# Head scores of a cross-conditioned attention layer as fp32 products in row quarters, in place of stacked high and low parts

## The chip, the cores and the metric

The kernel runs on one core of a Trainium2 chip. The metric is the device time of one execution in microseconds (us); three executions were timed. The engines are called PE (TensorE, with PEld its weight loads), DVE (VectorE), ACT (ScalarE), POOL (GpSimd) and SP (SyncE).

## What is computed

The input x is 64 sequences x 128 positions x 512 features, float32. It goes through two layers; only the second is changed. Its core, from the reference (16 heads of 32 features, B = 64, T = 128):

```python
xn = layer_norm(x, norm_w, norm_b)
q = (xn @ q_w + q_b).reshape(Bx, Tx, H, -1)
k = (xn @ k_w + k_b).reshape(Bx, Tx, H, -1)
att = jnp.einsum('bnhl,bmhl->bnmh', q, k)
att = att + (1.0 - mask) * -1000000.0
att = jax.nn.softmax(att, axis=2)
v = ((xn @ v_w + v_b) * src_mask[:, :, None]).reshape(Bx, Tx, H, -1)
y = jnp.einsum('bnmh,bmhl->bnhl', att, v).reshape(Bx, Tx, Dx)
h = layer_norm(y, sb_norm_w, sb_norm_b) * (1.0 + scale) + shift
return x + jax.nn.silu(h) @ out_w + out_b
```

The first layer has the same frame around a linear attention of 8 heads.

## The kernel before

A setup stage prepares weights, layer 1 (`layer0`) runs over 32 pairs of sequences, then layer 2 (`layer1`) does. Every engine has its own program, written out by hand; semaphores join them (`wait_ge`, `then_inc`). Layer 2 is a software pipeline: `body(i)` projects pair i and finishes pair i - 1. There are 32 bodies and an end for the last pair. b is the sequence in the pair, c a chunk of 128 features (four heads), a the head's place in its chunk, which is also its quarter of 32 partitions.

Each projection is three passes (`project_rows` L457 to L450, `project_features`; PE rows L448 to L450 and L457 to L459): high times high, low times high, high times low, in fp32r. Twelve matmuls make one projection of 512 columns (values or output, of one sequence) and twelve of 256 columns one chunk of the keys or queries of both.

The head scores use the same three parts, but one head has only 32 features, so the parts are stacked on the partitions. `qk_high` (ACT, L1302) takes each chunk of keys and queries out of PSUM as fp32r, and `qk_low` (DVE, L1168) what is left of it. 25 DMAs of a pair (`restack` on SP, `query_low_rows` on ACT) copy the parts into `stack`: high, high and low of the keys against high, low and high of the queries, 96 rows, then two rows of the mask and one of the shift. One matmul of 98 rows by 128 columns then gives a head's scores with its mask (`scores`, L1498). DVE takes the negated row maxima (`maxima`, L1176, each over one PSUM bank of four heads). `shift_row` (L1508) transposes them, ACT copies them and a DMA puts them in row 98 of the stack (`shift_out`). `weight_scores` (L1456) computes the scores a second time, keys on the partitions, shifted by the maximum, and `exps` (ACT, L1315) makes the weights out of them. So each pair has 2 x 16 matmuls of scores and 2 x 16 of weight scores, 128 x 128 each.

`mixed` (L1465, L1471) applies the weights: fp32 products with 32 output partitions, four at once in the column quarters of the array. `turned` (L1482), `z_transposed` (L1415) and `x_transposed` (L1405) transpose.

PE's order in a body: keys 0 and 1, with `shift_row` of sequence 1 of the previous pair in between; weight scores of sequence 0; keys 2 and 3; weight scores 1; queries 0 and 1; `mixed` 0; queries 2 and 3; `mixed` 1; values 0 (with `turned` between); z 0; values 1 (with x transposes); z 1; then the scores and the two output projections woven matmul by matmul. Scores of sequence 1 go to the same banks as those of sequence 0, so they wait for the maxima; DVE alternates maxima with its other work.

## Time and profile before

| | us |
|---|---|
| three timed runs: lowest, median, highest | 2303.02, 2305.43, 2308.46 |
| the profiled execution | 2304.43 |
| its span in the trace | 2302.6 |
| PE busy in the span | 2232.5 (97%) |
| DVE busy | 1458.1 (63%) |
| ACT busy | 871.8 (38%) |
| POOL busy | 569.1 (25%) |

The busy time of PE is modelled at the ends of matmuls, which overlap, so a stream is read from the starts of its rows in the timeline, not from their durations. In the 40 slices of the page PE is at 9 tenths or more in nearly all of them, in both layers. The chain that ended last is PE for 48% of the span in named rows, and no other engine has more than 2%.

### The profile page before, as it was taken

To read this page: it belongs to the slowest core of one execution; us is meant where nothing else is said; L and a number is where in the kernel's file an instruction comes from. 1 tells how busy PE (TensorE), PEld (TensorE's weight loads), DVE (VectorE), ACT (ScalarE), POOL (GpSimd) and SP (SyncE) were. 2 spreads that over 40 slices of the span, in tenths; PEclk is the share of its full clock that TensorE was granted. 3 is DMA by queue.
4 is the path that set the end of the run, shared out by engine and by line. 5 is a ranking of instruction groups with operands and counts; after the bars stand their busy time and mean duration, and the time that the engine had idled before them with its cause. 6 is when DMAs were issued, how large, how long until landed. Compare 5 with 4: busy or idle time off the path is not lost.

```text
span 2302.6 us, 49399 instructions
## 1 busy us (share of the span) xinstructions
PE 2232.5 (97%) x18430; PEld 1953.2 (85%) x18430; DVE 1458.1 (63%) x3127; ACT 871.8 (38%) x2021; POOL 569.1 (25%) x847
## 2 busy tenths in 40 slices
PE   6999999999999999995999999999999999999997
PEld 2888888888888888884989898989898988888886
DVE  4677777777777777745565656565656565555554
ACT  2333333333333333322344444444444444444443
POOL 0332223333333333313212121212122121212120
PEclk9999999999999999987999999999999999999998
DMA  7201111110100011003354444444444535353532
GB/s 247 86 32 37 37 37 37 37 37 37 37 30 34 32 37 37 32 24 88 81 123 105 116 112 114 114 107 117 107 122 101 128 101 129 94 129 92 129 87 72
DMA packets 90934, 187.17 MB, mean 81 GB/s; under 512 B 18708, under 2 KB 29394, under 8 KB 90904
## 3 DMA queue, kind: packets, MB, share of 16 engines
q1 hardware_dynamic: 82712, 169.44, 26.9%
q10 hardware_dynamic: 8192, 17.31, 3.2%
q8 instruction: 20, 0.33, 0.1%
q14 instruction: 10, 0.08, 0.0%
HBM read 51.81 MB, written 33.69 MB: 37 GB/s over the span
## 4 chain that ended last, share of the span: by engine, by line
PE 48%; ACT 2%; DVE 2%; SPq 1%; DMA 1%; issue 1%; POOL 0%; DVEq 0%; POOLq 0%
PE bank L457 6%; PE bank L459 5%; PE bank L458 5%; PE bank L1456 5%; PE bank L449 5%; PE bank L448 5%; PE bank L450 5%; PE bank L1498 4%; PE bank L1465 3%; PE bank L1471 2%; PE bank L1482 1%; SPq L1052 1%; PE bank L1405 1%; PE bank L1415 1%; ACT g L1332 1%; DMA stack<-parts 1%
## 5 line engine op out<-in xcount | busy, mean ns | idle before, releaser
L457 PE MATMUL bank<-xT_hi,w_hi 128*128 128x256 f32 x1536 | 444.7, 290 | 2.6 <-DVE xT_lo L1159 1.4
L458 PE MATMUL bank<-xT_lo,w_hi 128*128 128x256 f32 x1536 | 441.6, 287 | 0.0
L459 PE MATMUL bank<-xT_hi,w_lo 128*128 128x256 f32 x1536 | 439.0, 286 | 0.0
L448 PE MATMUL bank<-w_hi,xT_hi 128*128 128x512 f32 x768 | 322.7, 420 | 0.0
L450 PE MATMUL bank<-w_lo,xT_hi 128*128 128x512 f32 x768 | 317.8, 414 | 0.0
L449 PE MATMUL bank<-w_hi,xT_lo 128*128 128x512 f32 x768 | 311.8, 406 | 0.0
L457 PEld LDWEIGHTS bank<-xT_hi,w_hi 128*128 128x128 f32 x1536 | 291.1, 189 | 10.8 <-issue 6.1
L1168 DVE SCALAR_TENSOR_TENSOR parts<-bank,qk_bias,parts 128x256 fp32r<-128x256 f32 x256 | 111.1, 475 | 294.4 <-ACT parts L1302 294.4
L458 PEld LDWEIGHTS bank<-xT_lo,w_hi 128*128 128x128 f32 x1536 | 292.3, 190 | 1.7
L459 PEld LDWEIGHTS bank<-xT_hi,w_lo 128*128 128x128 f32 x1536 | 291.4, 190 | 0.0
L448 PE MATMUL bank<-w_hi,h_hi 128*128 128x512 f32 x512 | 217.6, 425 | 3.6 <-DVE h_lo L1218 3.6
L449 PE MATMUL bank<-w_hi,h_lo 128*128 128x512 f32 x512 | 215.8, 421 | 0.0
L805 ACT ACTIVATE k_exp<-bank,k_neg 128x128 f32<-128x128 f32 x256 | 73.0, 370 | 370.7 <-DVE k_neg L690 368.7
L1498 PEld LDWEIGHTS bank<-stack 98*128 98x128 f32 x1024 | 173.9, 194 | 46.4 <-DVE top L1176 21.1
L450 PE MATMUL bank<-w_lo,h_hi 128*128 128x512 f32 x512 | 210.4, 411 | 0.0
L1302 ACT ACTIVATE parts<-bank,qk_bias 128x256 fp32r<-128x256 f32 x256 | 107.5, 471 | 236.2 <-PE bank L459 236.2
L1498 PE MATMUL bank<-stack 98*128 98x128 f32 x1024 | 172.5, 268 | 10.1 <-DMA stack<-parts 8.1
L450 PEld LDWEIGHTS bank<-w_lo,xT_hi 128*128 128x128 f32 x768 | 144.6, 188 | 39.5
L1108 POOL TENSOR_TENSOR xr<-xr,bias_all 128x512 f32 (+1 forms) x64 | 81.1, 1289 | 392.3 <-DVE top L1176 391.4
L448 PEld LDWEIGHTS bank<-w_hi,xT_hi 128*128 128x128 f32 x768 | 144.6, 188 | 38.9 <-DVE parts L1168 6.2
L1176 DVE TENSOR_REDUCE top<-bank 128x4 f32<-128x512 f32 x256 | 169.9, 683 | 9.1 <-PE bank L1498 9.0
L449 PEld LDWEIGHTS bank<-w_hi,xT_lo 128*128 128x128 f32 x768 | 145.2, 189 | 30.5
(173 smaller groups left out, 4191.9 us busy)
## 6 DMA issues: line engine op xcount, KB each, us to landing
stack<-parts SPq DMA_DIRECT2D x640, 128.0 KB
xr<-in_x SPq DMA_DIRECT2D x32, 512.0 KB, 3.5
x_between_layers<-x SPq DMA_DIRECT2D x64, 256.0 KB, 2.0
xr<-x_between_layers SPq DMA_DIRECT2D x32, 512.0 KB, 3.6
stack<-parts ACTq DMA_DIRECT2D x128, 128.0 KB
out<-y_out SPq DMA_DIRECT2D x64, 256.0 KB, 2.0
raw<-in_L_cond_W_emb SPq DMA_DIRECT2D x4, 1024.0 KB, 12.2
raw<-in_L_cond_emb_w SPq DMA_DIRECT2D x4, 1024.0 KB, 7.6
```

The source lines that it names most:

```text
L448: yield nc.tensor.matmul(bank[:, :], a_hi[:, c, b, :], w_hi[:, m, c, :], start=(c == 0), stop=False)
L449: yield nc.tensor.matmul(bank[:, :], a_lo[:, c, b, :], w_hi[:, m, c, :], start=False, stop=False)
L450: yield nc.tensor.matmul(bank[:, :], a_hi[:, c, b, :], w_lo[:, m, c, :], start=False, stop=(c == C - 1))
L457: yield nc.tensor.matmul(dst, w_hi[:, m, c, fs], a_hi[:, c], start=(first and c == 0), stop=False)
L458: yield nc.tensor.matmul(dst, w_hi[:, m, c, fs], a_lo[:, c], start=False, stop=False)
L459: yield nc.tensor.matmul(dst, w_lo[:, m, c, fs], a_hi[:, c], start=False, stop=(c == C - 1))
L1108: last = nc.gpsimd.tensor_tensor(xr[:, slot, b], xr[:, slot, b], bias_all[:, BO, :], ALU.add)
L1168: nc.vector.scalar_tensor_tensor(parts[:, LO[n], c].rearrange("p b t -> p (b t)"), ps[QK_BANKS[n][c // 2]][:, at:at + PAIR * P], qk_bias[: ...
L1176: nc.vector.tensor_reduce(top[:, b, :].rearrange("p (a c) -> p a c", c=C)[:, :, j], ps[S_BANKS[j]][:, :].rearrange("p (h t) -> p h t", h=H ...
L1302: nc.scalar.activation(parts[:, HI[n], c].rearrange("p b t -> p (b t)"), ps[QK_BANKS[n][c // 2]][:, at:at + PAIR * P], ACT.Identity, bias= ...
L1456: last = nc.tensor.matmul(ps[W_BANKS[j]][:, a * P:(a + 1) * P], stack[0:K_SHIFTED, 1, a, j, b, :], stack[0:K_SHIFTED, 0, a, j, b, :], star ...
L1498: last = nc.tensor.matmul(ps[S_BANKS[j]][:, a * P:(a + 1) * P], stack[0:K_SCORE, 0, a, j, b, :], stack[0:K_SCORE, 1, a, j, b, :], start=Tr ...
```

## The change

The keys and queries are taken out of PSUM once each, in full fp32, into `qk`: the keys by DVE (`keys_out`), the queries by ACT (`queries_out`). A head's scores are one fp32 matmul of 32 rows by 128 columns, read from the partitions where the projection left the head, in the row quarter `tile_position=(DH * a, 0)` of the array (`heads`). The four heads of a chunk, in four quarters, write to four banks. A bank now holds one quarter's four heads. The mask is added first, by one matmul per bank with two rows of ones against `mask_rows`, 512 columns wide; the shift likewise, by four rows of ones against `top_T`, which ACT writes in four copies, each with a column of zeros and ones (`chunk_of`) as its scale. In the weight scores the mask is the bias of the exponentials (`mask_add`). The `stack`, its DMAs and `qk_low` are gone. `top` is padded to 128 columns, so the transposed maxima lie in the quarters.

The order changes too. The first scores follow z 0, ahead of values 1. The second scores stand between the two output projections, as a block. Nothing is woven there. The transposes of x stand before output projection 0 and after it. The banks of values, z, outputs and shift rows change with it. DVE normalises the next pair before it takes out the keys; `keys_out` waits until the weight scores of the previous pair are done. The setup gets one transpose and one copy (`mask_off`).

The core of the diff (waits and names around it follow in kind; `exps`, `maxima` and `mixed` keep their number of instructions):

```diff
-    parts = sb(ctx, "parts", [P, 4, C, PAIR, P], F32R)
-    Q_LO, Q_HI, K_HI, K_LO = range(4)
-    HI, LO = (Q_HI, K_HI), (Q_LO, K_LO)
-
-    stack = sb(ctx, "stack", [P, 2, HC, C, PAIR, P], F32R)
+    qk = sb(ctx, "qk", [P, 2, C, PAIR, P])
+    mask_rows = sb(ctx, "mask_rows1", [P, PAIR * P], F32R)
+    mask_add = sb(ctx, "mask_add", [P, PAIR])
+    one_rows = sb(ctx, "one_rows", [P, P], F32R)
+    chunk_of = sb(ctx, "chunk_of", [P, DH])
     v = sb(ctx, "v1", [P, PAIR, H, DH])
     one_col = sb(ctx, "one_col", [P, C, DH])
-    top = sb(ctx, "top", [P, PAIR, H])
-    top_T = sb(ctx, "top_T", [H, PAIR, P], F32R)
+    top = sb(ctx, "top", [P, PAIR, P])
+    top_T = sb(ctx, "top_T", [P, PAIR, C, P], F32R)
...
-    V_BANKS = (2, 3)
+    V_BANKS = (4, 6)
     S_BANKS = (0, 1, 2, 3)
     S_ORDER = ((0, 1, 2, 3), (2, 3, 0, 1))
-    Z_BANKS = (4, 5)
-    O_BANKS = (4, 5)
+    Z_BANKS = (5, 4)
+    O_BANKS = (5, 4)
     X_BANKS = (7, 6)
-    T_BANKS = (7, 6)
-    Z_AFTER = 11
+    T_BANKS = (7, 0)
...
-            def rows(side, part, r):
-                for a in range(HC):
-                    sp.dma_start(f32(stack[DH * r:DH * r + DH, side, a]),
-                                 f32(parts[DH * a:DH * a + DH, part])).then_inc(s["stack"], 16)
...
+        def load_masks(pair):
+            for a in range(HC):
+                sp.dma_start(f32(mask_rows[DH * a:DH * a + 2, :]),
+                             mask_d[1, :, bass.ds(pair * PAIR, PAIR)].rearrange("r b t -> r (b t)"))\
+                    .then_inc(s["masks_in"], 16)
...
+        def keys_out(i, first):
+            if not first:
+
+                dve.wait_ge(s["w_ps"], seq(PAIR * C, i - 1, PAIR * C))
+            for c in range(C):
                 if c % 2 == 0:
-
-                    dve.wait_ge(s["qk_hi"], seq(2 * C, i, (1 - n) * C + c + 2))
+                    dve.wait_ge(s["qk_ps"], seq(C, i, c // 2 + 1))
                 at = (c % 2) * PAIR * P
-                nc.vector.scalar_tensor_tensor(
-                    parts[:, LO[n], c].rearrange("p b t -> p (b t)"), ps[QK_BANKS[n][c // 2]][:, at:at + PAIR * P],
-                    qk_bias[:, n, c:c + 1], f32(parts[:, HI[n], c]).rearrange("p b t -> p (b t)"), ALU.add,
-                    ALU.subtract).then_inc(s["qk_lo"], 1)
+                done = nc.vector.tensor_scalar(qk[:, K, c].rearrange("p b t -> p (b t)"),
+                                               ps[QK_BANKS[K][c // 2]][:, at:at + PAIR * P], qk_bias[:, K, c:c + 1],
+                                               None, ALU.add)
+                if c % 2:
+                    done.then_inc(s["k"], 1)
...
         def body(i, first, more, last):
-            qk_low(i, 1, range(C))
             if not last:
                 row_stats(i + 1, (i + 1) % RING)
-            qk_low(i, 0, (0, 1))
+                norm(i + 1, (i + 1) % RING)
+            keys_out(i, first)
             if not first:
                 end_outputs(i - 1, 0)
-            qk_low(i, 0, (2, 3))
-            if not last:
-                norm(i + 1, (i + 1) % RING)
-            if not first:
                 end_norm(i - 1, 0)
                 end_outputs(i - 1, 1)
...
+        def exps(prev, b):
+            if b == 0:
+                act.wait_ge(s["mask_add"], seq(1, prev, 1))
             for a in range(HC):
-                act.dma_start(f32(stack[DH:2 * DH, 0, a]),
-                              f32(parts[DH * a:DH * a + DH, Q_LO])).then_inc(s["stack"], 16)
-
-        def exps(prev, b):
-            for j in range(C):
-                act.wait_ge(s["w_ps"], seq(PAIR * C, prev, b * C + j + 1))
-                nc.scalar.activation(prob[:, b, HB * j:HB * j + HB, :],
-                                     ps[W_BANKS[j]][:, :].rearrange("p (h t) -> p h t", h=HB),
-                                     ACT.Exp).then_inc(s["prob"], 1)
+                act.wait_ge(s["w_ps"], seq(PAIR * C, prev, b * C + a + 1))
+                nc.scalar.activation(prob[:, b].rearrange("p (c a) t -> p c a t", c=C)[:, :, a, :],
+                                     ps[W_BANKS[a]][:, :].rearrange("p (c t) -> p c t", c=C),
+                                     ACT.Exp, bias=mask_add[:, b:b + 1]).then_inc(s["prob"], 1)
...
         def shift_out(i, b):
             act.wait_ge(s["top_ps"], seq(PAIR, i, b + 1))
-            nc.scalar.activation(top_T[:, b, :], ps[T_BANKS[b]][0:H, 0:P], ACT.Copy).then_inc(s["top_T"], 1)
-            act.wait_ge(s["top_T"], seq(PAIR, i, b + 1))
-            act.dma_start(f32(stack[ROW_SHIFT:ROW_SHIFT + 1, 0, :, :, b, :]).rearrange("o a c t -> o (a c) t"),
-                          f32(top_T[:, b, :])).then_inc(s[f"shift{b}"], 16)
-
+            for c in range(C):
+                done = nc.scalar.activation(top_T[:, b, c, :], ps[T_BANKS[b]][:, 0:P], ACT.Copy,
+                                            scale=chunk_of[:, c:c + 1])
+            done.then_inc(s["top_T"], 1)
...
+        def heads(dst, weights, moving, b, order, signal):
+
+            for c in range(C):
+                for a in order:
+                    rows = slice(DH * a, DH * a + DH)
+                    last = nc.tensor.matmul(ps[dst[a]][:, c * P:(c + 1) * P], qk[rows, weights, c, b, :],
+                                            qk[rows, moving, c, b, :], start=False, stop=(c == C - 1),
+                                            tile_position=(DH * a, 0))
+                    if c == C - 1:
+                        last.then_inc(signal, 1)
+
         def weight_scores(prev, b):
...
-            pe.wait_ge(s[f"shift{b}"], seq(16, prev, 16))
-            for j in range(C):
-                if b == 0 and j < 2:
-
-                    pe.wait_ge(s["out"], seq(PAIR, prev, j + 1))
-                if b == 0 and j == 2:
-
-                    pe.wait_ge(s["top_T"], seq(PAIR, prev, PAIR))
-                if b == 1:
-                    pe.wait_ge(s["prob"], seq(PAIR * C, prev, j + 1))
-                for a in range(HC):
-                    last = nc.tensor.matmul(ps[W_BANKS[j]][:, a * P:(a + 1) * P], stack[0:K_SHIFTED, 1, a, j, b, :],
-                                            stack[0:K_SHIFTED, 0, a, j, b, :], start=True, stop=True)
-                last.then_inc(s["w_ps"], 1)
+            pe.wait_ge(s["top_T"], seq(PAIR, prev, b + 1))
+            if b == 0:
+
+                pe.wait_ge(s["out"], seq(PAIR, prev, PAIR))
+            else:
+                pe.wait_ge(s["prob"], seq(PAIR * C, prev, C))
+            for a in range(HC):
+                rows = slice(DH * a, DH * a + C)
+                nc.tensor.matmul(ps[W_BANKS[a]][:, :], one_rows[rows, :],
+                                 top_T[rows, b].rearrange("p c t -> p (c t)"), start=True, stop=False,
+                                 tile_position=(DH * a, 0))
+            heads(W_BANKS, K, Q, b, range(HC), s["w_ps"])
...
-        def scores(i, b, banks):
+        def scores(i, b, first):
 
             if b == 0:
-                pe.wait_ge(s["stack"], seq(16 * STACK_DMAS, i, 16 * STACK_DMAS))
-            for j in banks:
-                if b == 0 and j >= 2:
-
-                    pe.wait_ge(s["v"], seq(PAIR, i, j - 1))
-                if b == 1:
-                    pe.wait_ge(s["top"], seq(PAIR * C, i, j + 1))
-                for a in range(HC):
-                    last = nc.tensor.matmul(ps[S_BANKS[j]][:, a * P:(a + 1) * P], stack[0:K_SCORE, 0, a, j, b, :],
-                                            stack[0:K_SCORE, 1, a, j, b, :], start=True, stop=True)
-                    if a == HC - 1:
-                        last.then_inc(s["s_ps"], 1)
-                    if a % 2:
-                        yield
+                pe.wait_ge(s["masks_in"], seq(16 * HC, i, 16 * HC))
+                pe.wait_ge(s["q"], seq(2, i, 2))
+                pe.wait_ge(s["k"], seq(2, i, 2))
+            else:
+                pe.wait_ge(s["top"], seq(PAIR * C, i, C))
+            for a in S_ORDER[b]:
+                rows = slice(DH * a, DH * a + 2)
+                nc.tensor.matmul(ps[S_BANKS[a]][:, :], one_rows[rows, :],
+                                 mask_rows[rows, b * P:(b + 1) * P].unsqueeze(1).broadcast_to([2, C, P]),
+                                 start=True, stop=False, tile_position=(DH * a, 0))
+            heads(S_BANKS, Q, K, b, S_ORDER[b], s["s_ps"])
...
-            woven(values1, () if last else x_transposed(i + 1, first))
+            scores(i, 0, first)
+            run(value_rows(i, 1, first))
             if first:
                 pe.wait_ge(s["preset"], 2)
-            outputs0, scores0 = () if first else out_rows(i - 1, 0), scores(i, 0, S_ORDER[0])
+            pe.wait_ge(s["v"], seq(PAIR, i, 1))
             if not first:
                 z_transposed(i - 1, 1)
-            run(islice(scores0, 4))
-            woven(outputs0, scores0)
-            outputs1, scores1 = () if first else out_rows(i - 1, 1), scores(i, 1, S_ORDER[1])
-            woven(outputs1, scores1, 6)
+            if not last:
+                x_transposed(i + 1, 0)
+            if not first:
+                run(out_rows(i - 1, 0))
+            if not last:
+                pe.wait_ge(s["v"], seq(PAIR, i, PAIR))
+                x_transposed(i + 1, 1)
+            scores(i, 1, first)
+            outputs1 = () if first else out_rows(i - 1, 1)
+            run(islice(outputs1, 6))
             if not last:
 
                 pe.wait_ge(s["xT_lo"], seq(PAIR, i + 1, 1))
             shift_row(i, 0)
-            woven(outputs1, scores1)
+            run(outputs1)
```

What stands on PE now and stood there before, at the second scores (a body of the loop). `bank<-stack` are head scores, `h_hi` and `h_lo` the activations of the output projection, `qk` keys and queries. Before:

```order
L448 MATMUL bank<-w_hi,h_hi 128x512 [waits l1_h_lo]
L1496 REGISTER_ALU
L1498 MATMUL bank<-stack 128x128 [waits l1_top]
L1498 MATMUL bank<-stack 128x128
L449 MATMUL bank<-w_hi,h_lo 128x512
L1498 MATMUL bank<-stack 128x128 x2
L450 MATMUL bank<-w_lo,h_hi 128x512
L1498 MATMUL bank<-stack 128x128 [waits l1_top]
L1498 MATMUL bank<-stack 128x128
L448 MATMUL bank<-w_hi,h_hi 128x512
L1498 MATMUL bank<-stack 128x128 x2
```

With the change:

```order
L1386 MATMUL bank<-ident,xn 128x128 x3
L1485 MATMUL bank<-mask_rows,one_rows 128x512 [waits l1_top]
L1485 MATMUL bank<-mask_rows,one_rows 128x512 x3
L1427 MATMUL bank<-qk 128x128 x16
L453 MATMUL bank<-w_hi,h_hi 128x512 [waits l1_h_lo]
L454 MATMUL bank<-w_hi,h_lo 128x512
L455 MATMUL bank<-w_lo,h_hi 128x512
L453 MATMUL bank<-w_hi,h_hi 128x512
L454 MATMUL bank<-w_hi,h_lo 128x512
L455 MATMUL bank<-w_lo,h_hi 128x512
L1493 MATMUL bank<-ident,top 128x128 [waits l1_top,l1_xT_lo]
```

Eight of the scores' matmuls stand here ahead of, and between, single matmuls of the output projection; with the change sixteen stand as one block ahead of it, behind four 512 columns wide, and wait for all maxima of sequence 0.

PE at the weight scores of sequence 0 before, the last row being the next keys:

```order
L1456 MATMUL bank<-stack 128x128 [waits l1_out,l1_shift0]
L1456 MATMUL bank<-stack 128x128 x3
L1456 MATMUL bank<-stack 128x128 [waits l1_out]
L1456 MATMUL bank<-stack 128x128 x3
L1456 MATMUL bank<-stack 128x128 [waits l1_top_T]
L1456 MATMUL bank<-stack 128x128 x7
L457 MATMUL bank<-xT_hi,w_hi 128x256 [waits l1_top]
L458 MATMUL bank<-xT_lo,w_hi 128x256
```

With the change, from the last matmul of keys 1:

```order
L464 MATMUL bank<-xT_hi,w_lo 128x256
L1443 MATMUL bank<-top_T,one_rows 128x512 [waits l1_out,l1_top_T]
L1443 MATMUL bank<-top_T,one_rows 128x512 x3
L1427 MATMUL bank<-qk 128x128 x16
L462 MATMUL bank<-xT_hi,w_hi 128x256 [waits l1_top]
```

The sixteen matmuls, until now in groups of four per bank, follow four of the shift.

DVE at the head of a loop body before (`ISA` and `REGISTER_ALU` rows work out semaphore values):

```order
L1168 SCALAR_TENSOR_TENSOR parts<-bank,qk_bias,parts 128x256 [waits l1_qk_hi]
L1168 SCALAR_TENSOR_TENSOR parts<-bank,qk_bias,parts 128x256
L1166 REGISTER_ALU
L1168 SCALAR_TENSOR_TENSOR parts<-bank,qk_bias,parts 128x256 [waits l1_qk_hi]
L1168 SCALAR_TENSOR_TENSOR parts<-bank,qk_bias,parts 128x256
L1142 ISA
L1144 ISA [waits l1_x_in]
L1144 BN_STATS stats<-xr 128x6
L1144 ISA
L1144 BN_STATS stats<-xr 128x6
L1145 ISA
L1146 COPY seen<-eps 128x1 [waits l1_stats]
```

With the change, from the end of the next pair's statistics:

```order
L1137 ISA
L1138 COPY seen<-eps 128x1 [waits l1_stats]
L1140 BN_AGGR mv<-stats 128x2 x2
L1144 REGISTER_ALU
L1146 TENSOR_SCALAR xn<-xr,mv,rstd 128x512 [waits l1_rstd]
L1146 TENSOR_SCALAR xn<-xr,mv,rstd 128x512
L1157 ISA
L1160 ISA [waits l1_w_ps]
L1162 TENSOR_SCALAR qk<-bank,qk_bias 128x256 [waits l1_qk_ps]
L1162 TENSOR_SCALAR qk<-bank,qk_bias 128x256
L1160 REGISTER_ALU
L1162 TENSOR_SCALAR qk<-bank,qk_bias 128x256 [waits l1_qk_ps]
```

The normalisation of the next pair, which waits for POOL's `rstd`, stands ahead of the keys now, and the keys wait for the previous weight scores; their low parts are gone.

## Rows read from the trace of the kernel before

**Rows 1.** The page: the span, and busy time, share and instructions of each engine.
```profile
span 2302.6 us, 49399 instructions
PE 2232.5 (97%) x18430; PEld 1953.2 (85%) x18430; DVE 1458.1 (63%) x3127; ACT 871.8 (38%) x2021; POOL 569.1 (25%) x847
```

**Rows 2.** A stretch: length; busy PE, PEld, DVE, ACT, POOL; PEclk; DMA; GB/s.
```profile
1400.00:1700.00 300.00, 299.47 (x2904) 268.28 (x2903) 173.42 (x358) 126.72 (x288) 63.28 (x104) 1.00 0.46 113
```

**Rows 3.** Timeline, PE (start, us, row): scores and output projections of a body.
```profile
1505.57 0.60 PE L1415 MATMUL bank<-ident,z 128*128 128x128 f32 x4
1506.00 1.11 PE L1498 MATMUL bank<-stack 98*128 98x128 f32 x8
...
1509.06 0.40 PE L450 MATMUL bank<-w_lo,h_hi 128*128 128x512 f32 x1
...
1510.70 0.40 PE L448 MATMUL bank<-w_hi,h_hi 128*128 128x512 f32 x1
...
1514.00 0.27 PE L1508 MATMUL bank<-ident,top 128*16 128x128 f32 x1
...
1515.96 0.28 PE L457 MATMUL bank<-xT_hi,w_hi 128*128 128x256 f32 x1
```

**Rows 4.** Timeline, PE: the weight scores, and the next body's shift row.
```profile
1518.94 1.90 PE L1456 MATMUL bank<-stack 99*128 99x128 f32 x16
1520.67 0.33 PE L457 MATMUL bank<-xT_hi,w_hi 128*128 128x256 f32 x1
...
1551.74 0.27 PE L1508 MATMUL bank<-ident,top 128*16 128x128 f32 x1
```

**Rows 5.** Timeline, PE, layer 1: fp32 products on the whole array, next row.
```profile
714.88 1.95 PE L950 MATMUL bank<-att,qT 128*128 128x130 f32 x16
716.83 0.38 PE L907 MATMUL bank<-mask_rows,key_bias 128*128 x1
```

**Rows 6.** Timeline, PE: fp32 products in column quarters, and the neighbours around them.
```profile
1528.13 0.28 PE L459 MATMUL bank<-xT_hi,w_lo 128*128 128x256 f32 x1
1528.34 1.08 PE L1465 MATMUL bank<-prob,v 128*32 128x128 f32 x32
1529.24 1.06 PE L1471 MATMUL bank<-prob,one_col 128*32 128x128 f32 x32
1530.22 0.38 PE L457 MATMUL bank<-xT_hi,w_hi 128*128 128x256 f32 x1
1530.45 0.28 PE L458 MATMUL bank<-xT_lo,w_hi 128*128 128x256 f32 x1
```

**Rows 7.** Groups by line: busy us, mean ns; idle before.
```profile
L1498 PEld LDWEIGHTS bank<-stack 98*128 98x128 f32 x1024 | 173.9, 194 | 46.4 <-DVE top L1176 21.1 <-issue 5.7 <-DMA stack<-parts 3.4
L1465 PEld LDWEIGHTS bank<-prob,v 128*32 128x32 f32 x2048 | 52.1, 109 | 8.6
```

**Rows 8.** Timeline, PEld, layer 1: loads of 64 columns into two column halves.
```profile
712.52 1.01 PEld L940 LDWEIGHTS bank<-v,k_rows 128*64 128x64 f32 x32 [0.36 <-issue]
```

**Rows 9.** Timeline, PE: waits for the stacked copies, first and last pair.
```profile
1091.95 6.74 PE L1498 MATMUL bank<-stack 98*128 98x128 f32 x28 [5.38 <-DMA stack<-parts]
...
2261.43 1.11 PE L1498 MATMUL bank<-stack 98*128 98x128 f32 x8 [1.08 <-DMA stack<-parts]
```

**Rows 10.** Timeline, PE, ACT and DVE: from transposed z to h_lo, one sequence.
```profile
1539.18 0.60 PE L1415 MATMUL bank<-ident,z 128*128 128x128 f32 x4
1539.81 1.51 ACT L1332 ACTIVATE g<-bank,gains 128x128 f32<-128x128 f32 x4 [3.19 <-PE bank L1415]
...
1543.44 0.69 DVE L1218 TENSOR_TENSOR h_lo<-hs,h_hi 128x512 fp32r<-128x512 f32 x1 [0.70 <-ACT h_hi L1342]
```

**Rows 11.** Page, groups by line: the maxima, out of PSUM.
```profile
L1176 DVE TENSOR_REDUCE top<-bank 128x4 f32<-128x512 f32 x256 | 169.9, 683 | 9.1 <-PE bank L1498 9.0
```

**Rows 12.** Timeline, POOL: its work behind the last maxima of a pair.
```profile
1516.12 2.54 POOL L1108 TENSOR_TENSOR xr<-xr,bias_all 128x512 f32 x2 [12.30 <-DVE top L1176]
...
1518.86 2.04 POOL L1115 TENSOR_TENSOR v_bias<-bias_all,mask_now 128x512 f32<-128x512 f32 x2
```

More of the change, by code:

```diff
@@ L335, in _ @@
             last.then_inc(cond_ps, 1)
+            pe.wait_ge(mask_step, 4)
+            nc.tensor.transpose(ps[EMB_BANKS[1]][:, 0:B], mask_in[:, 1, :], ident[0:B, 0:B]).then_inc(mask_ps, 1)
             pe.wait_ge(vec_ready, 1)
@@ L1117, in biases, with mask_column @@
             last.then_inc(s["v_bias"], 1)
+        def mask_column(pair, first):
+            if not first:
+                pool.wait_ge(s["prob"], seq(PAIR * C, pair - 1, PAIR * C))
+            nc.gpsimd.tensor_copy(mask_add[:], mask_off[:, bass.ds(pair * PAIR, PAIR)]).then_inc(s["mask_add"], 1)
+        nc.gpsimd.memset(f32(one_rows[:]), 1.0).then_inc(s["rows_preset"], 1)
         norm(0)
-        pool.wait_ge(s["rstd"], 1)
-        nc.gpsimd.memset(f32(stack[ROW_MASK:ROW_MASK + 3]), 1.0).then_inc(s["rows_preset"], 1)
-        pool.wait_ge(s["rows_preset"], 1)
         def body(i, first, more, last):
@@ L1132, in body @@
                 end_rstd(i - 1, 1)
+            mask_column(i, first)
         bodies(pool, NP, body)
@@ L1229, in _ @@
         row_stats(0, 0)
+        nc.vector.memset(top[:], 0.0)
+        nc.vector.reduce_sum(chunk_of[:], ident[:].rearrange("p (a r) -> p r a", a=HC), AX_X)
         nc.vector.memset(one_col[:], 0.0).then_inc(s["preset"], 1)
@@ L1397, in _, with x_transposed @@
     def _(pe):
-        def x_transposed(pair, first):
-            for b in range(PAIR):
-                pe.wait_ge(s["xn"], seq(PAIR, pair, b + 1))
-                if not first:
-                    pe.wait_ge(s["y"], seq(PAIR, pair - 2, PAIR))
-                for c in range(C):
-                    last = nc.tensor.transpose(ps[X_BANKS[b]][:, c * P:(c + 1) * P], xn[:, b, c * P:(c + 1) * P],
-                                               ident[:])
-                    if c == C - 1:
-                        last.then_inc(s["xT_ps"], 1)
-                    yield
+        def x_transposed(pair, b):
+            pe.wait_ge(s["xn"], seq(PAIR, pair, b + 1))
+            for c in range(C):
+                last = nc.tensor.transpose(ps[X_BANKS[b]][:, c * P:(c + 1) * P], xn[:, b, c * P:(c + 1) * P], ident[:])
+            last.then_inc(s["xT_ps"], 1)
         def z_transposed(prev, b):
@@ L1433, in projected, with value_rows @@
                     done.then_inc(s["qk_ps"], 1)
-        def value_rows(i, b):
-            pe.wait_ge(s["qk_lo"], seq(2 * C, i, 2 * (b + 1)))
+        def value_rows(i, b, first):
+            if not first:
+                pe.wait_ge(s["y"], seq(PAIR, i - 1, b + 1))
             done = None
@@ L1531, in body @@
                 mixed(i - 1, 1)
-            values0 = value_rows(i, 0)
+            values0 = value_rows(i, 0, first)
             run(islice(values0, 4))
```

117 lines of the change are left out of this document (50 added, 67 removed).

## The prediction

> **What bounds the kernel now.** I read the page first: PE is busy for 97% of the span, DVE for 63% [rows 1]. Then a stretch of layer 2 by itself: in 300 us PE is busy for 299.5, DVE for 173 and ACT for 127, at a granted clock of 1.00 [rows 2]. So layer 2 is as long as what PE has to issue. The next two views are PE's timeline. One `shift_row` stands at 1514.00 and the next at 1551.74 [rows 3, 4]: a body takes 37.74 us. The reader should see in the rows between them what each step takes from start to start, for the durations overlap. An output projection issues seven matmuls in 1.64 us, 0.234 each, for 512 columns [rows 3]. The first 24 matmuls of the next body and a transpose take 2.98 us [rows 3, 4], so one of 256 columns takes 0.12. Four transposes take 0.43 [rows 3].
>
> **What the scores cost now.** From the transposes of z to the next body there are 10.39 us [rows 3]. Less the transposes (0.43), 24 output matmuls (5.62) and the shift row (0.11), 4.23 us are left for the 32 first scores. The weight scores take 1.73 us for sixteen [rows 4], 3.46 for both sequences. Together 7.69 us of each body. Sixteen in 1.73 is 0.108 each, though 128 columns at 0.12 for 256 would be 0.06: here the weight load of 128 columns sets the pace. At 0.108, 32 first scores would be 3.46, so 0.77 of their 4.23 is waiting. Most of that has a row: PEld waited 21.1 us in all for `top`, 0.66 per pair [rows 7].
>
> **What a block of scores costs after the change.** There are four per pair. Each holds four matmuls of 512 columns (mask or shift) and sixteen heads, in rounds of four quarters. No row of this trace shows a product in a row quarter, so each part comes from the nearest row.
> - *A round of four heads.* The nearest row is the same product turned by 90 degrees: fp32, 128 columns, four at once in column quarters. Thirty-two of them take 0.90 us [rows 6], 0.1125 a round. On the whole array with 128-column weights, an fp32 product of 130 columns takes 1.95/16 = 0.122 [rows 5]. So fp32 costs twice the time of fp32r per column, and the load of 128 columns hides behind it. Four rounds: 0.45. The other end is no overlap of the quarters at all: sixteen times 0.108 [rows 4], 1.73.
> - *Are the loads concurrent?* A head loads 128 columns, where a column quarter loads 32. The two lengths are 194 and 109 ns [rows 7], 0.89 ns a column, so 64 columns need about 57 ns. In layer 1, 32 loads of 64 columns, in two column halves, stand in 1.01 us [rows 8], 28 ns from start to start. Loads to different parts of the array overlap there. I take the same for rows; it is the one assumption that the result hangs on.
> - *The wide matmuls.* At best four at once, 0.234 [rows 3]; at worst one after another, 0.94. I take 0.234, by the same assumption.
> - *Entering and leaving the tiled form.* From the last 256-column matmul before the column quarters to the second after them is 2.32 us [rows 6]. Less sixteen rounds (1.80) and two matmuls (0.24), 0.28 are left. A load of 128 columns in place of 32 adds 0.085 [rows 7]: 0.37.
>
> Sum of a block: 0.37 + 0.234 + 0.45 = 1.05 us, 4.2 for a pair instead of 7.69: 3.49 less.
>
> **What the order adds.** Nothing is woven now, so each wait has to be covered by whole steps.
> - *Output projection 0* waits for `h_lo`. That chain takes 4.95 us now, from the start of z's transposes to the end of `h_lo` (1539.18 to 1544.13) [rows 10]. After the change, z 0, a block, values 1, z 1 and x 0 stand in between: 0.43 + 1.05 + 2.81 + 0.43 + 0.43 = 5.15. But DVE has two maxima and a normalisation inside the chain, 0.68 a maximum [rows 11], and any of them can be in the way. I take 0.25 us of stall, between 0 and 0.7.
> - *Second scores* wait for all four maxima of sequence 0. Since the first block PE has values, three sets of transposes and a projection, 6.9 us. DVE has eight operations, about 5.4 at 0.68. Covered by 1.5.
> - *Weight scores 1* wait for all four exponentials of sequence 0; keys 2 and 3 (2.9 us) cover them by some 0.5. *Weight scores 0* wait for the last `end_add`, 2.9 us of keys behind it. Covered.
> - *POOL and DVE at the head of a body.* POOL's biases start when the maxima are in and end 4.8 us later [rows 12]. `rstd` comes behind them, so DVE stands in `norm` for some 6 us and then takes out the keys, with whatever stands behind them. The first taker on PE is the first scores, some 21 us into the body. If the cover went, a late key would cost PE one for one.
> - *ACT* gets six more copies a pair, for the eight of `shift_out` replace two, and loses the four chunks of keys; it has 127 busy of 300 us [rows 2]. DVE loses eight operations and gets four. SP loses 21 DMAs a pair and gets four small ones, due a body later; ACT's queue loses six. The padded shift rows may cost 0.05 each: 0.1 a pair.
>
> So a body loses 3.49 - 0.35 = 3.14 us: 34.6 instead of 37.74. Times 32: 100 us.
>
> **The ends.** With the stack go PE's waits for it in the first and last pair, 5.38 and 1.08 us [rows 9]. The setup gets a transpose and a copy, some 0.3, and the last pair's weight scores wait for exponentials. Together with what these waits delay I take 8 us less, between 4 and 14, since what stood behind them moves up too. Sum: 2302.6 - 100 - 8 = 2194.6 of span, 2196.4 for that execution, and the median of the three runs is 1 us above it: **2197 us**.
>
> **The rivals.**
> - *Overlap, but incomplete.* The quarters' results go to four banks at once, which no row shows. If a round is 1.3 times as long, so are the wide ones: a block gets 0.13 + 0.07 us longer, a pair 0.8, and the time is 2197 + 26 = 2223. For it: nothing. Against it: column quarters lose almost nothing [rows 6], but they share one bank. The Trainium skill ("TensorE: Matmul & The Clock Gate", table of measured speedups in Part 3) has 3.07 times for four row quarters of 512 columns instead of 4, which is this factor of 1.3. Chance 0.11.
> - *A quarter can't load while it multiplies.* Then a round is a load and a product in turn, 0.225 us, a block is 1.50, a pair 1.8 longer: 2255. Against it: the scores now load 128 columns for 194 ns in the very rows that are multiplying, and still start each 0.108 [rows 4, 7]. The same skill page ("The mechanism", Part 3) says that a load overlaps a running matmul only where the row group differs; by the rows this isn't so on the whole array. The page "FP8 and Floating Point Precision" ("TensorE Precision Notes") gives fp32 four passes, which would come to about the same time; the trace shows two times the fp32r time [rows 5, 6]. Chance 0.08.
> - *The block order stalls PE.* If the `h_lo` chain comes 0.7 late, and the shift row or the next keys wait another 0.7 for maxima that DVE reaches late, a body is 1.2 longer than forecast: 2235. DVE's 173 of 300 us speak against it [rows 2]. Chance 0.05.
> - *The quarters take turns* (the other side). If weights of different row groups come in over one path, sixteen loads of 128 columns stay sixteen times 0.108, and the wide matmuls come one by one: 0.37 + 0.94 + 1.73 = 3.04 a block, 12.2 a pair against 7.69 now. A body is 4.8 longer with the stall: 2304.4 + 155 - 8 = 2451. It decides from about 80 ns per head upwards: there a block reaches 1.9 us and the gain is gone. For it: a head has the same 128 columns to load and to stream as now, so without overlap nothing is saved, and the trace shows overlap for columns alone. Chance 0.11.
>
> **How the numbers follow.** The forecast has the remaining 0.65. The range goes down to 2165: no stall at all (11 us), tiled form entered and left for half the price (24). Up it takes in incomplete overlap, stalls and the doubled round, with 10 us over: 2265. Only the quarters that take turns lie outside. About 0.2% is what a measurement of this kernel tells from no change. Slower is the last rival, 0.11; that the cases should meet at no change, 0.02; faster 0.87.
>
> **What would show it.** PE's timeline should have blocks of 1.05 us: four wide matmuls within a few ns of each other, then sixteen heads over 0.45, in steps of four per 0.11. Shift rows of one kind should stand 34.6 us apart. `parts` and `stack` are gone, DVE waits for `rstd` at a body's head, and the granted clock stays at 1.00 in layer 2. PE's wait before output projection 0 is under 0.7. If a head starts each 0.03 us and the time is above 2230, PE's waits on DVE were misjudged; if a head starts each 0.06 or 0.11, the assumption on the row quarters was wrong, and the time says by how much.

## The result and the profile after

| | before | with the change |
|---|---|---|
| median of the timed runs, us | 2306.94 (2303.02 to 2309.18) | 2240.9 (2240.46 to 2241.82) |
| span of the profiled execution | 2302.6 | 2240.0 |
| one body of layer 2 | 37.74 | 35.98 |

The ratio is 0.9716, with a 95% interval of 0.9699 to 0.9733. The kernel is faster, and the time lies in the range; but the gain is 66 us where 108 were forecast. The change was run again beside the second set of experiments:

> The change itself, on the same chip as the three beside it: 2241 us.

Measured: 2239.93 us, ratio 0.9716 (0.9702 to 0.9729).

The page of the changed kernel, to read beside [rows 1]:

```profile
span 2240.0 us, 53652 instructions
PE 2180.2 (97%) x20991; PEld 1883.2 (84%) x20991; DVE 1400.3 (63%) x3001; ACT 906.7 (40%) x2086; POOL 549.0 (25%) x879
```

And its stretch of layer 2, beside [rows 2] (length; busy PE, PEld, DVE, ACT, POOL; PEclk; DMA; GB/s):

```profile
1400.00:1700.00 300.00, 300.00 (x3646) 262.91 (x3646) 174.16 (x347) 141.90 (x319) 60.72 (x115) 1.00 0.08 29
```

PE is still the bound, and more so: 300.00 of 300 us busy at full clock. The instruction count of PE rose from 18430 to 20991, which is the first thing that doesn't fit: per pair the program has 64 head matmuls as before, 16 wide ones and nothing else new. That makes 512 more, and the setup has one transpose more, but the count rose by 2561. The other 2048 are in the next view. It is PE's timeline (start, us, row) with the shift rows of two bodies and one block of weight scores, beside [rows 3, 4, 6]:

```profile
1517.63 0.27 PE L1493 MATMUL bank<-ident,top 128*128 128x128 f32 x1
...
1521.98 0.28 PE L464 MATMUL bank<-xT_hi,w_lo 128*128 128x256 f32 x1
1522.20 0.50 PE L1443 MATMUL bank<-top_T,one_rows 4*128 4x512 f32 x4
1522.53 1.06 PE L1427 MATMUL bank<-qk 32*128 32x128 f32 x32
1523.53 0.38 PE L462 MATMUL bank<-xT_hi,w_hi 128*128 128x256 f32 x1
1523.75 0.28 PE L463 MATMUL bank<-xT_lo,w_hi 128*128 128x256 f32 x1
...
1553.61 0.27 PE L1493 MATMUL bank<-ident,top 128*128 128x128 f32 x1
```

Sixteen head products stand as 32 rows. The groups by line (busy us, mean ns of one) say the same: 64 sequences x 2 x 16 heads are 2048 products, and the trace has

```profile
L1427 PE MATMUL bank<-qk 32*128 32x128 f32 x4096 | 136.7, 271 | 0.0
L1427 PEld LDWEIGHTS bank<-qk 32*128 32x128 f32 x4096 | 137.0, 187 | 4.8
```

Then the same count has to be made for the rows of before that I took the price from. `mixed` issues 16 matmuls of each kind per sequence, 1024 in all, and layer 1 issues four products of 130 columns per sequence, 256 in all. Groups by line of the kernel before:

```profile
L1465 PE MATMUL bank<-prob,v 128*32 128x128 f32 x2048 | 69.2, 276 | 0.0
L950 PE MATMUL bank<-att,qT 128*128 128x130 f32 x512 | 62.8, 275 | 0.5 <-DVE att L725 0.5
```

Twice the number, too. Every fp32 product is two rows, each with a weight load of its own. A timeline row "x32" was sixteen products, and I had read it as 32.

**Where the 62.6 us of span came from.** Three stretches between the same `shift_row` (of sequence 0) of the first and the last pair. Timeline of before, then of the changed kernel (the end with what PE waits for in brackets):

```profile
1098.49 0.41 PE L1508 MATMUL bank<-ident,top 128*16 128x128 f32 x1
...
2268.84 0.27 PE L1508 MATMUL bank<-ident,top 128*16 128x128 f32 x1
```

```profile
1085.16 0.33 PE L1493 MATMUL bank<-ident,top 128*128 128x128 f32 x1
...
2200.71 0.27 PE L1493 MATMUL bank<-ident,top 128*128 128x128 f32 x1
2203.32 0.51 PE L1443 MATMUL bank<-top_T,one_rows 4*128 4x512 f32 x4 [0.78 <-DVE y_out L1222]
...
2207.34 0.80 PE L1443 MATMUL bank<-top_T,one_rows 4*128 4x512 f32 x4 [2.63 <-ACT prob L1305]
...
2211.16 1.08 PE L1453 MATMUL bank<-prob,v 128*32 128x128 f32 x16 [1.31 <-ACT prob L1305]
```

Up to the first: 13.3 us less (1098.49 to 1085.16). Two things went with the stack. One is its fill in the setup. Timeline of POOL and DVE before, then DVE with the change, with the first normalisation of layer 2:

```profile
1055.61 7.68 DVE L1154 TENSOR_SCALAR xn<-xr,mv,rstd 128x512 f32<-128x512 f32 x2 [0.75 <-POOL rstd L1100]
1055.63 6.92 POOL L1122 MEMSET stack<- 3x8192 f32 x1
```

```profile
1056.74 1.01 DVE L1146 TENSOR_SCALAR xn<-xr,mv,rstd 128x512 f32<-128x512 f32 x2 [0.30 <-POOL rstd L1088]
```

Beside POOL's fill of 6.92 us DVE takes 7.68 us for what takes it 1.01 with the change, and PE's first row of layer 2 stands at 1062.89 before and at 1057.35 now, 5.5 us earlier. (The run below that keeps the stack has the 7.68 us, too; no run takes out the fill alone.) The other 7.8 us hold the wait of 5.38 us for the stacked copies [rows 9] and the clock behind it, less some waits that only the change has (twice 0.5 us). Before, PE is busy for 1.62 of the 7 us up to 1092.00, and from there to 1098.50 the granted clock is 0.50, the lower of its two levels (1.2 GHz in place of 2.4): its first 28 matmuls of scores take 6.5 us, where sixteen in the loop take 1.73. With the change the clock is 1.00 at its first scores.

Thirty-one bodies: 1170.35 us before, 1115.55 now, 54.8 less, 1.77 each. Behind the last: 33.8 before, 39.3 now, 5.5 more; PE waits there for `end_add` (0.78) and twice for exponentials (2.63 and 1.31), with no keys of a next pair as cover. Sum: 62.6.

### The profile page after: what moved, and what is told of

Read it like the earlier page. It is cut to its first block, busy times and chain, and to the rows that moved or that the text cites. A ratio compares the mean times of both kernels' runs of the same rounds, so it can differ in the third digit from the quotient of the medians.

```text
span 2240.0 us, 53652 instructions
## 1 busy us (share of the span) xinstructions
PE 2180.2 (97%) x20991; PEld 1883.2 (84%) x20991; DVE 1400.3 (63%) x3001; ACT 906.7 (40%) x2086; POOL 549.0 (25%) x879
## 4 chain that ended last, share of the span: by engine, by line
PE 51%; DVE 1%; ACT 0%; issue 0%; DMA 0%; POOL 0%; POOLq 0%; DVEq 0%; SPq 0%
PE bank L462 6%; PE bank L453 6%; PE bank L463 6%; PE bank L464 5%; PE bank L455 5%; PE bank L454 5%; PE bank L1427 5%; PE bank L1453 3%; PE bank L1459 3%; PE bank L1470 2%; PE bank L1443 1%; PE bank L1393 1%; PE bank L1386 1%; PE bank L1485 1%; PE bank L1493 0%; ACT prob L1305 0%
## 5 line engine op out<-in xcount | busy, mean ns | idle before, releaser
L455 PE MATMUL bank<-w_lo,xT_hi 128*128 128x512 f32 x768 | 309.7, 403 | 0.0
L454 PE MATMUL bank<-w_hi,xT_lo 128*128 128x512 f32 x768 | 306.6, 399 | 0.0
L454 PE MATMUL bank<-w_hi,h_lo 128*128 128x512 f32 x512 | 206.9, 404 | 0.0
L455 PE MATMUL bank<-w_lo,h_hi 128*128 128x512 f32 x512 | 203.5, 397 | 0.0
L1305 ACT ACTIVATE prob<-bank,mask_add 128x512 f32<-128x512 f32 x256 | 154.9, 688 | 100.1 <-PE bank L1427 100.1
L1136 DVE BATCH_NORM_STATS2 stats<-xr 128x6 f32 (+1 forms) x64 | 41.2, 685 | 186.8 <-DMA xr<-x_between_layers 186.5
L1322 ACT ACTIVATE g<-bank,gains 128x128 f32<-128x128 f32 x256 | 96.1, 456 | 142.3 <-PE bank L1393 142.3
L606 POOL TENSOR_TENSOR h_lo<-hs,h_hi 128x512 fp32r<-128x512 f32 x64 | 86.9, 1379 | 236.9 <-ACT h_hi L836 236.9
```

The source lines that it names most:

```text
L454: yield nc.tensor.matmul(bank[:, :], a_lo[:, c, b, :], w_hi[:, m, c, :], start=False, stop=False)
L455: yield nc.tensor.matmul(bank[:, :], a_hi[:, c, b, :], w_lo[:, m, c, :], start=False, stop=(c == C - 1))
L606: nc.gpsimd.tensor_tensor(h_lo[:, :, b, :], hs[:, b], f32(h_hi[:, :, b, :]), ALU.subtract).then_inc(s["h_lo"], 1)
L1305: nc.scalar.activation(prob[:, b].rearrange("p (c a) t -> p c a t", c=C)[:, :, a, :], ps[W_BANKS[a]][:, :].rearrange("p (c t) -> p c t", c=C),
L1322: last = nc.scalar.activation(g[:, b, c, :], ps[Z_BANKS[b]][:, c * P:(c + 1) * P], ACT.Identity, scale=gains[:, 0, c, b:b + 1], bias=gains ...
```

## The experiments

Times are medians; the change itself is at 2241 or, in the second set, at 2240. All came with runs of the kernel before on the same chip (2305.5 to 2308).

### Head products in fp32r

```diff
-    qk = sb(ctx, "qk", [P, 2, C, PAIR, P])
+    qk = sb(ctx, "qk", [P, 2, C, PAIR, P], F32R)
```

> The change with the keys and queries in fp32r instead of fp32, so the head products are single-pass and their low parts are left out of the result; nothing else differs. Theory A (the prediction counted an fp32 product as one traced matmul, while each is two rows of 0.11 us: 32 rows for 16 heads): a block shows 16 head rows in four steps of 0.11, 0.44 us less than now, 1.78 a pair, 57 us in all: 2184 us. Theory B (a quarter cannot load weights while it multiplies): the number of rows stays 32, or the steps stay eight long for sixteen rows, about 2240 us. Theory C (weight loads of different quarters queue up): 16 rows 0.1 us apart, 1.7 us a block, slower than 2300 us.

Measured: 2185.93 us, ratio to before 0.9474 (0.9458 to 0.9489). Timeline of PE, one block:

```profile
1505.37 0.51 PE L1443 MATMUL bank<-top_T,one_rows 4*128 4x512 f32 x4
1505.71 0.57 PE L1427 MATMUL bank<-qk 32*128 32x128 f32 x16
1506.21 0.39 PE L462 MATMUL bank<-xT_hi,w_hi 128*128 128x256 f32 x1
```

Sixteen rows for sixteen heads, and from the first head to the next keys 0.50 us, where the change has 1.00 (1522.53 to 1523.53). Four blocks are 2.0 us shorter, but a body (34.2 us between shift rows) only 1.8: ahead of output projection 0 PE now stands 0.2 us, for `h_lo` (PEld waits 6.1 us for it in all). Twice the rows for fp32 is worth 55 us of the kernel's time. That is the whole distance between 2241 and the forecast of 2197, and 11 us more. Theory A holds. Theories B and C fall: a quarter loads the next weights while it multiplies, and the quarters' loads of 128 columns run side by side.

### Quarter by quarter

```diff
-            for c in range(C):
-                for a in order:
+            for a in order:
+                for c in range(C):
```

> The same products as the change, but all four heads of one quarter in a row, then the next quarter. Theory A (four quarters work at once, and a quarter's own load hides behind its product): 32 rows one after another at 0.11 us, 3.5 us instead of 0.89 a block, 2.65 more for each of 128 blocks: 2241 + 340 = 2580 us. If a load could not hide behind the product of its own quarter: 0.21 us a row, 6.8 a block, about 3000 us. If the overlap of quarters had brought nothing: 2241 us.

Measured: 2477.85 us, ratio 1.0738 (1.0717 to 1.076). Timeline of PE, one block:

```profile
1505.63 0.51 PE L1485 MATMUL bank<-mask_rows,one_rows 2*128 2x512 f32 x4
1505.96 2.71 PE L1427 MATMUL bank<-qk 32*128 32x128 f32 x32
1508.61 0.50 PE L453 MATMUL bank<-w_hi,xT_hi 128*128 128x512 f32 x1
```

The heads take 2.65 us to the next step instead of 1.00, 1.65 more; 128 times that is 211 of the 237 us. My 2580 was too high: strictly one row after another would be 3.5 us, and it was 2.65. The starts in the trace show why. Rows of one quarter start 0.11 us apart, though each has a load of its own of 187 ns, so a load does hide behind the product of its own quarter. But the next quarter's first row starts with the fifth of the eight rows of this quarter (at 1506.41 both), so three rows run beside the next quarter's: 23 steps of 0.11 instead of 32.

The other 25 us are the clock. Of the bodies, 17 take 44.08 us instead of 42.59. In one of them, behind the weight scores of sequence 1 (timeline of PE, then a stretch with the clock behind POOL's busy time):

```profile
1317.16 0.41 PE L464 MATMUL bank<-xT_hi,w_lo 128*128 128x256 f32 x1
1317.38 0.41 PE L462 MATMUL bank<-xT_hi,w_hi 128*128 128x256 f32 x1
```

```profile
1316.00:1318.00 2.00, 2.00 (x11) 2.00 (x11) 0.73 (x2) 0.00 (x0) 0.00 (x0) 0.50 0.00 0
```

The granted clock is 0.50. Most of the 24 projections of the queries stand 0.21 us apart instead of 0.12, and all of them take 4.56 us instead of 3.07: 1.49 us in each of 17 bodies. The profile has PE busy all through; ahead of the fall it had worked through two blocks with one quarter after another. In the change, where the same products rotate, every body takes 35.98 us and the clock is 1.00. So the order of issue is worth 237 us, three and a half times what the whole change brings, and a tenth of it comes through the clock.

### No mask products ahead of the first scores

```diff
-            for a in S_ORDER[b]:
-                rows = slice(DH * a, DH * a + 2)
-                nc.tensor.matmul(...)
-            heads(S_BANKS, Q, K, b, S_ORDER[b], s["s_ps"])
+            heads(S_BANKS, Q, K, b, S_ORDER[b], s["s_ps"], True)
```

(`True` lets the first product of each bank start the accumulation.)

> The four 512-column mask products ahead of the first scores are left out (64 of 128 blocks), so the maxima are taken over unmasked scores; the exponentials keep the mask. They take 0.336 us a block by the trace, against the 0.234 of the prediction. If they cost that on the path: 0.67 us a pair, 21 us less: 2220 us. If the head products only waited for weights that load behind the wide ones, a part of it stays as load time: down to 14 us less, 2227.

Measured: 2227.35 us, 13.6 less than the change. Timeline of PE, the second scores and their neighbours:

```profile
1505.27 0.39 PE L455 MATMUL bank<-w_lo,h_hi 128*128 128x512 f32 x1
1505.50 0.60 PE L1386 MATMUL bank<-ident,xn 128*128 128x128 f32 x4
1506.02 1.17 PE L1427 MATMUL bank<-qk 32*128 32x128 f32 x32
1507.13 0.50 PE L453 MATMUL bank<-w_hi,h_hi 128*128 128x512 f32 x1
```

From the first row of the block to the output projection it is 1.11 us here, and 1.33 with the wide ones (1522.20 to 1523.53): 0.22 less, times 64 is 14. The second expectation holds: of the 0.33 us between wide and head rows, 0.11 stays. Without the wide matmuls it stands behind the first round of heads (the second starts 0.21 us after it, not 0.11), which fits a weight load at the entrance that somebody has to pay.

### Second scores woven into output projection 1

```diff
-            scores(i, 1, first)
+            scores1 = scores(i, 1, first)
+            run(islice(scores1, 1))
             outputs1 = () if first else out_rows(i - 1, 1)
-            run(islice(outputs1, 6))
+            woven(outputs1, scores1, 6)
```

(`scores` here yields after each chunk.)

> The second scores go between single matmuls of output projection 1 again, a round of four heads at a time: four tiled stretches where there was one. Theory A (each change between the whole array and the quarters costs 0.3 us): three more pairs of changes, 0.9 us a pair of sequences, 29 us: 2270 us. Theory B (changes cost nothing, the 0.3 is the fill of the first product): 2241 us. If the later scores make PE wait for maxima, up to 15 us on top.

Measured: 2284.27 us, 43 more than the change, which leaves 23 of its 66 us. Timeline of PE:

```profile
1527.75 0.39 PE L1427 MATMUL bank<-qk 32*128 32x128 f32 x8
1528.20 0.50 PE L453 MATMUL bank<-w_hi,h_hi 128*128 128x512 f32 x1
1528.63 0.50 PE L1427 MATMUL bank<-qk 32*128 32x128 f32 x8
1529.06 0.49 PE L454 MATMUL bank<-w_hi,h_lo 128*128 128x512 f32 x1
...
1530.79 0.51 PE L453 MATMUL bank<-w_hi,h_hi 128*128 128x512 f32 x1
```

Eight rows of heads should take 0.22 and an output matmul 0.234; they take 0.45 and 0.43. Three more entrances and exits cost 43/32 = 1.35 us a pair, 0.45 each and not 0.3. PE has no wait for maxima, but some of this is `h_lo` (PEld waited 7.2 us for it in all). So unwoven order and quarters belong together. The old order wove both scores, in more stretches than this run; with the quarters it was not run, but an estimate from 0.45 us a stretch leaves little or nothing of the gain.

### The scores in blocks, with the stack

```diff
-            run(islice(scores0, 4))
-            woven(outputs0, scores0)
+            run(scores0)
+            run(outputs0)
...
-            woven(outputs1, scores1, 6)
+            run(scores1)
+            run(islice(outputs1, 6))
...
-            maxima(i, 0, (0,))
+            maxima(i, 0, (0, 1, 2, 3))
```

(The other three calls of `maxima` for sequence 0, between other work, are gone; the four maxima are now taken together. The first scores stay behind values 1 and z 1, and the transposes of x stay woven, so this is the change's blocks and not the whole of its order.)

> The kernel before with the order of the change alone: first scores as one block, output projection 0, second scores as one block, output projection 1; DVE takes the four maxima of sequence 0 without other work between. Products, stack and copies are those of before. Theory A (a large part of the change's gain, 0.77 of 1.76 us a body, is that PE no longer waits for maxima): up to 0.7 us a body less, 2307 - 22 = 2285. Theory B (all of it is the products): 2307. If the copies of the stack are late for a block that needs them all at once: slower.

Measured: 2292.08 us, ratio 0.994 (0.9926 to 0.9953). Timeline of PE:

```profile
1506.54 1.90 PE L1494 MATMUL bank<-stack 98*128 98x128 f32 x16
1508.27 0.44 PE L448 MATMUL bank<-w_hi,h_hi 128*128 128x512 f32 x1
...
1509.72 0.27 PE L1504 MATMUL bank<-ident,top 128*16 128x128 f32 x1
...
1546.88 0.27 PE L1504 MATMUL bank<-ident,top 128*16 128x128 f32 x1
```

A block of sixteen takes 1.73 us, as the weight scores always did, and the body 37.16 instead of 37.74. PE waits for no maxima. So 13 us, a fifth of what the change gains, could be had by the order without row quarters. Per body it is 0.58 of 1.76, a third; of the 18 us that this makes in all bodies, the first and last pair take 5 back. That the two parts simply add up wasn't tested.

### The load of x ahead of the wait for the stored output

```diff
-                sp.wait_ge(s["stored"], seq(16 * PAIR, i - 1, 16 * PAIR))
             if more:
                 sp.wait_ge(x_in, seq(16, i, 32))
                 load_rows(sp, x1_d, xr, i + 2, (i + 2) % RING, x_in)
+            if not first:
+                sp.wait_ge(s["stored"], seq(16 * PAIR, i - 1, 16 * PAIR))
```

> In the change DVE stands idle 6.4 us at each body's head until the rows of x have landed, for SP issues the load behind the wait for the stored output. Here the load is issued ahead of that wait. Theory A (PE has some 20 us of cover for all that hangs on DVE's head of body): DVE's wait falls by about 2 us a body and the time stays at 2241. Theory B (the late keys or norms reach PE somewhere): up to 2 us a body, 60 us less.

Measured: 2241.87 us beside 2239.93 for the change: no gain. The waits of the change (us in total, times, longest us) and of this kernel:

```profile
DVE stats L1136 <- DMA xr<-x_between_layers: 186.5, 29, 6.7
```

```profile
DVE stats L1137 <- DMA xr<-x_between_layers: 144.0, 29, 5.2
```

This wait was not in the prediction, which has DVE stand for `rstd` there, some 6 us; for that it waits 1.1 us a body. It was new, 6.4 us in each body, since `row_stats` moved ahead of the keys, and SP sends the load only when the last output is stored. It fell by a quarter, 1.5 us a body, and nothing came of it: what hangs on DVE's head of body is covered, as forecast.

### First scores directly behind `mixed`

```diff
                 mixed(i - 1, 1)
+            scores(i, 0, first)
             values0 = value_rows(i, 0, first)
...
-            scores(i, 0, first)
             run(value_rows(i, 1, first))
```

> The first scores stand directly behind the mixed products of sequence 1 (column quarters), ahead of values 0, so that the array changes from column quarters to row quarters without a stretch of full-array products between. Theory A (a change costs by the drain and the load at each side, some 0.2 us, whichever forms meet): one change of five or six a body is saved, 0.2 us, 6 us in all: 2235. Theory B (column to row quarters is as dear as two changes): 2241. If the queries come out of PSUM too late, PE waits and it is slower.

Measured: 2275.64 us, 36 more than the change. Timeline of PE, then the z transposes in the groups by line (after the bar, the idle time before them):

```profile
1515.80 1.06 PE L1459 MATMUL bank<-prob,one_col 128*32 128x128 f32 x32
1516.79 0.51 PE L1485 MATMUL bank<-mask_rows,one_rows 2*128 2x512 f32 x4
...
1518.12 0.50 PE L453 MATMUL bank<-w_hi,xT_hi 128*128 128x512 f32 x1
...
1525.71 0.63 PE L1393 MATMUL bank<-ident,z 128*128 128x128 f32 x4 [0.53 <-DVE z L1204]
```

```profile
L1393 PE MATMUL bank<-ident,z 128*128 128x128 f32 x256 | 39.8, 279 | 21.8 <-DVE z L1204 21.8
L1393 PEld LDWEIGHTS bank<-ident,z 128*128 128x128 f32 x256 | 29.5, 141 | 39.1 <-issue 28.9 <-DVE z L1204 6.0
```

By the time, neither theory: the sign is wrong. The block between z 0 and values 1 had also covered the way of z of sequence 1 (turned, statistics, POOL's `rstd`, normalisation). With the block gone from there, PE reaches z 1 too soon and stands 0.5 us, its loads 0.9: from the last matmul of values 1 (1524.79) to the transposes it is 0.92 us instead of 0.23. Output projection 0 then waits for `h_lo`, 0.28 us a body (PEld, 8.5 us in all). The two make 0.97 of the 1.03 us by which a body grew. I had looked only at whether the queries would be late. The cheaper meeting of column and row quarters can still be read from the rows. Here the block takes 1.33 us from its first wide matmul to values 0, with `mixed` ahead of it and the values behind it as long as without it; between full-array products it costs 1.53. That is the 0.2 us of theory A. It is lost again ahead of values 1, where PEld now waits 0.18 us for DVE.

### Maxima from fp32r scores, weights from fp32 scores

```diff
+    qk_r = sb(ctx, "qk_r", [P, 2, C, PAIR, P], F32R)
...
+                for to in (qk, qk_r):
...
-            heads(S_BANKS, Q, K, b, S_ORDER[b], s["s_ps"])
+            heads(S_BANKS, Q, K, b, S_ORDER[b], s["s_ps"], qk_r)
```

(The loop over `to` writes the keys on DVE and the queries on ACT, into both tiles.)

> The change with a second, fp32r copy of keys and queries; the first scores (of which only the maxima are kept) read that copy, single-pass, the weight scores stay fp32. Nothing is left out: a rounded maximum shifts numerator and sum alike. Four more operations a pair on DVE and four on ACT, 0.42 us each. Theory A (head rows are what a pass costs, and both engines have cover): first blocks show 16 head rows over 0.44 us less, 0.88 a pair, 28 us in all: 2240 - 28 = 2212 us. Theory B (the extra operations reach PE through the queries or the copies behind them): up to 0.8 us a body back, 2238 us.

Measured: 2217.68 us, ratio to before 0.9609 (0.9596 to 0.9623). Timeline of PE, a block of first scores and one of weight scores:

```profile
1506.10 0.56 PE L1430 MATMUL bank<-qk_r 32*128 32x128 f32 x16
1506.59 0.51 PE L453 MATMUL bank<-w_hi,h_hi 128*128 128x512 f32 x1
...
1513.00 1.06 PE L1430 MATMUL bank<-qk 32*128 32x128 f32 x32
1514.00 0.39 PE L462 MATMUL bank<-xT_hi,w_hi 128*128 128x256 f32 x1
```

The first scores take 0.49 us, the weight scores 1.00. Shift rows stand 35.20 us apart, 0.78 less than in the change where I expected 0.88. The two blocks give 1.00 us, and 0.2 comes back as PE's wait for `h_lo` ahead of output projection 0 (PEld, 6.1 us in all), as in the run with fp32r heads. This beats both kernels and keeps the weights' own scores in fp32.

## Why the prediction was right, and where its size was off

- **What bounds it: right.** PE before and after.
- **Cost of the scores now, 7.69 us of a body: right.** Bodies went from 37.74 to 35.98. Of the 0.77 us of waiting in it, the run with the scores in blocks gives back 0.58. Four blocks of 1.53 now stand in the place of 7.69, and what is left of the body is 29.9 us, against 30.05 before.
- **A round of four heads, 0.1125 us: wrong by a factor of two, and this is the step that failed.** I divided 0.90 us by 32 products, and 1.95 us by 16, where the trace's count is in rows, and an fp32 product is two rows. A round takes 0.22, four of them 0.89 instead of 0.45. Four blocks of 32 pairs: 0.44 x 128 = 56 us too little. The fp32r run, with half the rows, is 55 us faster.
- **The rest of a block: right.** Forecast 0.37 at the edges and 0.234 for the wide matmuls, 0.60; measured 1.77 us from the last 256-column row before the block to the second behind it, less two of those (0.24) and 0.89 of heads: 0.64. The load at the entrance shows between the wide and the head rows, not before them.
- **The quarters work at once, loads included: right**, by the fp32r run and the one quarter by quarter. It was the assumption on which all hung.
- **The order: 0.35 us a body forecast, none measured.** It was 0.25 of stall before output projection 0 and 0.1 for the padded shift rows. PE has no idle in layer 2's loop, and a shift row with the matmul behind it takes 0.34 us, as before. The stall itself was well judged: it shows, with 0.2 us a body, in both runs whose first block is as short as I had forecast. In the change the block is 0.45 us longer and covers the `h_lo` chain.
- **The ends: forecast 8 us less, measured 7.8** (13.3 less at the start, 5.5 more at the end), and the agreement is luck. Of the start only the wait for the stack was forecast. The 5.5 us of the first normalisation, beside POOL's fill of the stack, and the half clock behind the wait were not, and neither was how long the last pair waits.
- **With the right count** the same sum gives 2197 + 58 = 2255; less the 0.35 a body, 11 us, it is 2244, and 2241 was measured.
- **The rival of the doubled round**, with a chance of 0.08, had the right price, 2255, and one of its two grounds was the true one: the Trainium skill ("FP8 and Floating Point Precision", "TensorE Precision Notes") gives true fp32 four passes. I set it aside with "the trace shows two times the fp32r time". With the products counted, a 130-column one takes 1.95/8 = 0.244 us against 0.059 for fp32r (130/512 of 0.234): four times. The trace agrees with the page. It doesn't follow that a head in fp32r costs a quarter: with a load of 128 columns for each product it costs half, 0.50 us a block against 1.00. The other ground, loads that can't overlap in their own row group, fell in the runs.
- **Incomplete overlap (2223)** was not it: the step between rounds of rows is 0.111 against 0.109 in the column quarters, and four wide matmuls cost 0.22 us by the run without them. **The block order that stalls PE** did not come either, and **the quarters that take turns** fell too.

## What to carry to other kernels

Before a duration is divided by the count in a trace, hold that count against the program's own: one instruction of the source can be several rows. When small products are packed in quarters, issue them in rotation over the quarters, keep them in one block, and pay for entering the tiled form once. And where a result serves only as a shift that cancels, a single-pass product will do for it.

## What was not expected of the hardware

- An fp32 product stands in the trace as two loads and two matmuls; 16 heads are 32 rows in steps of 0.111 us for four. In fp32r they are 16 rows in the same steps, but for the first (0.06). One pass of 128 columns would be done in about 0.06 (256 take 0.12), so in fp32r the weight load of 128 columns (0.108 apart in the old scores, too) seems to set the step. In fp32 the product alone would give it, too: in the column quarters, where a load has 32 columns, the step is 0.109. No run tells apart which of the two sets it in the row quarters.
- Sixteen heads in rotation over the quarters take 0.89 us, quarter by quarter 2.65. The slow order also had the granted clock fall to 0.50 behind it in 17 bodies, though PE had not stood still.
- A row-quarter block between full-array matmuls costs about 0.3 us beside its own rows (1.53 less 0.34 for the wide ones and 0.89), 0.2 less where it follows the column quarters, and each further stretch 0.45 when single matmuls stand between.
- Two DVE instructions took 7.68 us beside a POOL fill of 6.92 us and 1.01 without it.
